# Retention layer with layer norms and a one-expert MLP on 8 cores: q/k transposes issued ahead of the value and gate projections, and four PSUM drains moved from ScalarE to VectorE

## What is computed

```python
x = L0_attn_hidden_states                     # (8, 4096, 1024) f32
x = x + attn(_layernorm(x), W_qkv, W_g, W_proj, decay)
x = x + ffn(_layernorm(x), ...)
# attn, 8 heads, dk 128, dv 256:
q, k, v = split(h @ W_qkv)                    # 1024, 1024, 2048 columns
q, k = rotary(q, scale), rotary(k, 1/scale)
ret = (q @ k.T * dk**-0.5 * decay_mask) @ v   # causal, decay[h]**(n-m)
g = ret per head;  normed = (g - mean) * rsqrt(var + eps)
out = (silu(h @ W_g) * normed) @ W_proj       # 2048 -> 1024
# ffn: layer norm, mean over the sequence, softmax over 8 experts,
# the best expert's relu(z @ W_down) @ W_up, times its probability
```

## Time and profile before

| | us |
|---|---|
| median of 2 timed runs | 3204.56 |
| lowest and highest of them | 3182.6, 3226.52 |
| the profiled execution, its own time | 3163.36 |
| its span, slowest core (first to last instruction) | 3161.8 |
| spans of the eight cores | 3135.9 to 3161.8 |
| busy on that core: TensorE, VectorE, ScalarE, GpSimd | 1665.8, 1191.3, 711.7, 137.6 |

### The profile page before, as it was taken

One profiled execution on the slowest core, in us unless ns is written; L12 is line 12 of the kernel. 1 busy time (PEld: TensorE's weight loads), 2 busy tenths in 40 slices (PEclk: granted clock), 3 DMA queues, 4 the chain that ended last, 5 costly groups with the idle time before them and its releaser, 6 DMA issues.

```text
span 3161.8 us, 28862 instructions; the slowest of 8 cores (3135.9 to 3161.8 us)
## 1 busy us (share of the span) xinstructions
PE 1665.8 (53%) x8174; PEld 839.0 (27%) x8174; DVE 1191.3 (38%) x2229; ACT 711.7 (23%) x1260; POOL 137.6 (4%) x208
## 2 busy tenths in 40 slices
PE   0056556564655656555656465565655565653133
PEld 0022222322232323222232223232322223232121
DVE  1013426161615243352616161524435261615433
ACT  0012322212231313232221223132323222231000
POOL 0100000000000000000000000000000000000100
PEclk9996778687777777776868677787767686876555
DMA  7882354545352543434454535253343444432476
GB/s 125 108 212 98 100 171 140 173 140 173 123 171 100 166 147 114 159 107 166 140 173 140 173 130 173 91 176 137 114 154 113 166 140 146 140 120 87 139 240 227
DMA packets 156946, 459.24 MB, mean 145 GB/s; under 512 B 14197, under 2 KB 26486, under 8 KB 146294
## 3 DMA queue, kind: packets, MB, share of 16 engines
q1 hardware_dynamic: 128694, 344.13, 33.3%
q0 software_dynamic: 18880, 46.14, 7.7%
q10 hardware_dynamic: 9216, 67.11, 5.5%
HBM read 432.17 MB, written 58.72 MB: 155 GB/s over the span
## 4 chain that ended last, share of the span: by engine, by line
PE 35%; DVE 19%; ACT 17%; DMA 16%; issue 10%; POOL 2%; DVEq 1%; ACTq 1%; SPq 0%; POOLq 0%
DMA wp<-wproj_bf 7%; PE PA L572 6%; DMA wqkvg_bf<-wqkvg 4%; PE PA L506 4%; PE PA L759 3%; PE PB L506 3%; PE PC L382 3%; PE PB L759 3%; PE PC L572 3%; ACT v_sb L582 2%; DMA outT<-out_sb 2%; PE PD L572 2%; DVE gst L697 2%; DVE gst L694 2%; ACT gate_sb L582 2%
## 5 line engine op out<-in xcount | busy, mean ns | idle before, releaser
L371 DVE TENSOR_TENSOR ao_sb<-qs_sb 128x1024 bf16<-128x1024 bf16 x64 | 44.3, 692 | 844.8 <-ACT qs_sb L368 821.0
L572 PE MATMUL PA<-wnb,lnx_sb 128*128 128x512 bf16 x1024 | 336.1, 413 | 49.0 <-ACT v_sb L582 27.4
L572 PE MATMUL PC<-wnb,lnx_sb 128*128 128x512 bf16 x512 | 213.4, 417 | 238.2 <-ACT v_sb L582 212.8
L759 PE MATMUL PA<-ggT_sb,wp 128*128 128x256 bf16 x1024 | 242.7, 327 | 142.7 <-DMA wp<-wproj_bf 109.7
L506 PE MATMUL PA<-wnb,lnx_sb 128*128 128x512 bf16 x512 | 171.5, 419 | 171.0 <-DMA wnb<-wqkvg_bf 155.9
L759 PE MATMUL PB<-ggT_sb,wp 128*128 128x256 bf16 x1024 | 242.2, 326 | 24.3 <-ACT pe_sc L770 24.3
L572 PE MATMUL PD<-wnb,lnx_sb 128*128 128x512 bf16 x512 | 210.6, 411 | 14.7 <-ACT v_sb L582 6.8
L506 PE MATMUL PB<-wnb,lnx_sb 128*128 128x512 bf16 x512 | 166.1, 408 | 3.3 <-ACT qbf L517 3.3
L759 PEld LDWEIGHTS PA<-ggT_sb,wp 128*128 128x128 bf16 x1024 | 107.7, 115 | 208.8 <-issue 182.2
L572 PEld LDWEIGHTS PA<-wnb,lnx_sb 128*128 128x128 bf16 x1024 | 101.5, 103 | 197.7 <-issue 106.0
L517 ACT ACTIVATE qbf<-PA 128x1024 bf16<-128x1024 f32 x32 | 32.8, 1024 | 500.6 <-PE PA L506 500.6
(11 more groups left out here) (215 smaller groups left out, 2699.5 us busy)
## 6 DMA issues: line engine op xcount, KB each, us to landing
wnb<-wqkvg_bf SPq DMA_DIRECT2D x384, 512.0 KB, 5.5
wp<-wproj_bf SPq DMA_DIRECT2D x256, 512.0 KB, 6.3
x<-xt ACTq DMA_DIRECT2D x16, 1024.0 KB, 4.9
tab<-tabs ACTq DMA_DIRECT2D x16, 1024.0 KB, 7.3
xp<-xp_sb ACTq DMA_DIRECT2D x16, 1024.0 KB, 8.4
x<-xp POOLq DMA_DIRECT2D x16, 1024.0 KB, 8.2
outT<-out_sb ACTq DMA_DIRECT2D x16, 1024.0 KB, 4.5
wqkvg_bf<-wqkvg POOLq DMA_DIRECT2D x12, 1024.0 KB, 9.4
```

The source lines that it names most:

```text
L371: S.op("vector", lambda E, a=a, b=b: E.tensor_tensor(xsq_fl[:, a:b], xbf_fl[:, a:b], xbf_fl[:, a:b], ALU.mult), reads=[xbf_fl[:, a:b]], wr ...
L572: S.op("tensor", lambda E, m=m, k=k, P=P, wb=wb: E.matmul(P, lnx_sb[:, k, m * 128:(m + 1) * 128], wb[:, k % 4, :], start=(k == 0), stop=(k ...
L759: S.op("tensor", lambda E, vtp=vtp, sub=sub, vt=vt, f=f, P=P, fo=fo: E.matmul(P[:, fo:fo + C], wp_sb[vtp % 4][:, sub, f * 128:(f + 1) * 12 ...
```

## The change

Two edits. The transposes of q and k of the next chunk are issued before its value and gate projections and no longer after them. The four drains of the transposed `gg_sb` use `trans_group`'s default, VectorE, and no longer ScalarE.

```diff
@@ ggt_proj_phase
                 dv_ = ggT_sb[:, vg * 8:(vg + 1) * 8, i * 128:(i + 1) * 128]
-                trans_group(srcs, dv_, drain="scalar")
+                trans_group(srcs, dv_)
@@ loop over chunks
             gn_phase(c)
             if c + 1 < NRUN:
+                qkt_phase(c + 1)
                 vgate_phase(c + 1)
-                qkt_phase(c + 1)
```

## The result

| | before | after |
|---|---|---|
| median of the timed runs, us | 3181.82 (10 runs) | 3291.68 (11 runs) |
| ratio, after to before | | 1.0315, 95% interval 1.0271 to 1.0359 |
| profiled execution, slowest core's span, us | 3161.8 | 3264.9 |

The account below looks back on a forecast made before the run. A chain changing engines bounds each chunk, with ScalarE's evictions waiting behind L714. 14 chunks × (6.9 − 0.4) + 3.7 + 8.9 = 103.6 us added gives about 3300 us, range 3240 to 3365.

Parts of the forecast that it names:

- The first value pair was free, and is not any more: TensorE's first value/gate projection pair ran beside VectorE's group norm; after the change it ends 1.6 us later than today's second.
- 10.6 us until the last pair ends, 3.7 back, so the cast is 6.9 late: Per chunk, 1.6 plus 9.0 us for an added pair, less 3.7 us of q/k drains before ScalarE casts next x.
- Copies at 0.69 us and not 1.22; 0.4 won a chunk: Each ggT drain on VectorE takes 0.69 us, starting projections 0.4 us earlier; 1.22 us copies would cost 1.0 us.
- Chunk 14 at 3.7, chunk 15 at 8.9: Added us in the last two chunks: 14 has no next cast; in 15 ggT copies stand behind VectorE's L807.
- Loads hidden, nothing won back: Third pair's weight loads cost nothing, though up to 5 us a chunk without cover; later work in the chunk recovers nothing.
- The signs to look for: L714 wait near 295 us, qT drain wait over 200, L553 some 7 a chunk, L572 PC a few tens, 0.69 us copies.
- The time: Whole kernel: 103.6 us added to the profiled 3163.36 gives 3267.0; bases including timed runs give 3308 and 3294, stated as 3300.
- Transposes fill the hole: Rival: ScalarE's q/k drains precede L714, so the first pair ends early; 52 us won, 3153 us; chance 0.03.
- only the 3.7 us of drains come back: In the filled-hole rival's sum, 15 chunks each win 3.7 us from q/k drains no longer preceding the next x cast.
- the half-speed start of a pair: Rival: TensorE's clock does not fall, shortening first and last pairs by 2.8 us together a chunk; 3258 us; chance 0.08.

## Why the prediction was right

- *The first value pair was free, and is not any more.* Shown. The wait for L711 stayed (295.0 for 295.6 us), TensorE's wait moved in front of the pair, and moving the drains alone turned +3.15% into −2.5%.
- *10.6 us until the last pair ends, 3.7 back, so the cast is 6.9 late.* Measured 45.32 − 38.65 = 6.67. By its terms: the first pair ends 1.55 us later than the second did before (1.6 taken), the added pair costs 9.0, the last pair ends 10.4 later (10.6), and 3.7 come back.
- *Copies at 0.69 us and not 1.22; 0.4 won a chunk.* The copy takes 691 ns. From cast to projection it was 15.33 before and is 15.08, so 0.25 won. The Trainium skill, "VectorE: DVE Perf Modes", section "The perf-mode tier table", allows a copy from PSUM up to twice the base rate. The trace agrees: 691 ns, where an f32 copy of half as many elements took 692 ns.
- *Chunk 14 at 3.7, chunk 15 at 8.9.* Measured 3.86 and 8.66. The 8.66 holds on all cores; for chunk 14 the same core of both profiles gives 2.7 to 3.9, so 3.86 is at the upper end.
- *Loads hidden, nothing won back.* The third pair starts 0.30 us after the second, released by an eviction and not by a load (1603.16). The stretch from projection to L714 is 117.6 for 117.4 us.
- *The signs to look for.* The wait for qT's drain is 197.8 us, just short of the 200 named, and the wait of L572 on PC fell to 9.8 us, below the few tens named. The others are as written.
- *The time.* The sum gave 3267.0 us for the like of the profiled execution before, and the profiled execution after took 3266.5. The step from there to 3300 rests on a base taken from three executions, and the median of ten was 3181.82 and not 3204.56; that 3291.68 lies so near 3300 is in part luck.

What was off is the rival on the other side. "Transposes fill the hole" was priced at 52 us of gain; the kernel that does it gains 2.5% of 3156.16, some 79 us. What failed there is the sentence that only the 3.7 us of drains come back: with the hole filled the second pair and the last one mostly run at the upper clock level, another 1.0 us each, so 2.1 us a chunk. The prediction counted the half-speed start of a pair only as a rival of the forecast (2.8 us a chunk; the kernel before spent 1.9 + 1.5 us above the 8.70 us of such a pair at 1.00), not as part of what a filled hole is worth.

## What to carry to other kernels

Each engine's queue was worked off here in the order in which the code issues, so a drain took on the wait of what stood ahead of it (18.3 us before L714). Before moving work to an earlier place, list for each engine what it then stands behind, not only what it then stands ahead of. Here the swap of two calls that share nothing but ScalarE took the kernel from 1.0315 to 0.975 of the time before. When a wait is removed, look at once for the next one on the same tile (here the reuse of the gate tile, behind the value evictions).

## What the runs showed that I had not expected

- A pair of matmuls that ended sooner went with a later cast: in 4 of 14 chunks the first value pair ended 0.9 us before L714 and not 1.4 after it, TensorE stood 2.2 us and not 0.30 before the second pair, whose mean clock was 0.69 and not 1.00, and the cast came 3.8 us later. The pause is not shown as the cause: on other cores 7 such second pairs kept 1.00, and the last pair was the slow one.
- The load of the Silu table started only when the data of the eviction behind it were free: 1.28 us on the path after a wait of 12 to 14 us in which ScalarE did nothing.
- With b1_rest and its store of 512 KB moved by 21 to 23 us into the stretch of the projection's loads, that stretch took 3.6 us more a chunk.
